# Rests of the query and up weights on GpSimd, gate columns and one scaling on ScalarE, and a new order of all steps, in a macaron transformer kernel

## What is computed

```python
x = x + 0.5 * _L0_ffn_ref(_layernorm(x), ...)
x = x + _L0_attn_ref(_layernorm(x), ...)
x = x + 0.5 * _L0_ffn_ref(_layernorm(x), ...)

def _L0_ffn_ref(x, ...):
    h = _rmsnorm(x, gamma1)
    q = (h @ Wq + bq).reshape(b, t, H, HD)                        # 16 heads of 16
    kv = ((h @ Wdown + bdown) @ Wup + bup).reshape(b, t, H, 2 * HD)  # 64 wide between
    k, v = jnp.split(kv, 2, axis=-1)
    att = softmax(jnp.einsum('bthd,btgd->bthg', q, k) / np.sqrt(HD))  # within one token
    x = x + (jnp.einsum('bthg,btgd->bthd', att, v).reshape(b, t, D) @ Wo + bo)
    h2 = _rmsnorm(x, gamma2)
    gate = softmax(h2 @ Wg + bg)
    return x + jnp.einsum('btd,edf,bte->btf', h2, We, gate)       # all 8 experts, dense

def _L0_attn_ref(x, ...):                                         # 8 heads of 32
    scores = jnp.einsum('bngh,bmgh->bnmg', q, k) / scale
    probs = softmax(scores, axis=-1)                              # over the heads
    return jnp.einsum('bnmg,bmgh->bngh', probs, v).reshape(b, n, d)
```

## Time and profile before

| | before |
|---|---|
| median of 3 runs | 992.51 us (992.35 to 993.81) |
| the profiled execution | 993.92 us, span of its profile 991.8 us |
| PE busy | 953.0 us (96%) |
| DVE busy | 854.7 us (86%) |
| POOL busy | 792.7 us (80%) |
| ACT busy | 642.2 us (65%) |
| granted clock of PE | 1.000 in every slice |

### The profile page before, as it was taken

The page is one execution under the profiler, slowest core; times in us unless marked ns, Lnnn a source line. Parts: engine busy times, 40 slices in busy tenths (PEclk is TensorE's granted clock), DMA queues, the critical chain, the costliest instruction groups (busy, mean ns, idle before and its releaser), DMA issues. The chain is left out here.

```text
span 991.8 us, 28114 instructions
## 1 busy us (share of the span) xinstructions
PE 953.0 (96%) x11052; PEld 755.2 (76%) x11052; DVE 854.7 (86%) x1388; ACT 642.2 (65%) x1287; POOL 792.7 (80%) x865
## 2 busy tenths in 40 slices
PE   8799999999999989999999999887999999999998
PEld 7678887888888866666666666456788888888886
DVE  6889999899785469999999999999998998898743
ACT  4677566565755467777877877776765765666542
POOL 6988887986885538999899999998778959968554
PEclk9999999999999999999999999999999999999999
DMA  7021000000000000000000000000000000000001
GB/s 226 3 76 45 2 2 2 2 2 2 2 1 1 1 1 2 2 2 2 1 2 2 2 1 2 2 1 2 2 2 22 23 3 22 2 24 22 2 23 42
DMA packets 8398, 14.45 MB, mean 15 GB/s; under 512 B 1993, under 2 KB 5964, under 8 KB 8270
## 3 DMA queue, kind: packets, MB, share of 16 engines
q1 hardware_dynamic: 8270, 12.67, 3.8%
HBM read 8.48 MB, written 4.19 MB: 13 GB/s over the span
## 5 line engine op out<-in xcount | busy, mean ns | idle before, releaser
L514 PE MATMUL psum<-we,h 128*128 128x512 f32 x1536 | 382.2, 399 | 1.6 <-DVE h L1219 1.6
L514 PEld LDWEIGHTS psum<-we,h 128*128 128x128 f32 x1536 | 280.9, 188 | 62.4 <-issue 1.7
L1422 ACT ACTIVATE late<-psum,gate 128x256 f32<-128x256 f32 x252 | 105.0, 469 | 104.2 <-PE psum L514 59.7
L1256 DVE SCALAR_TENSOR_TENSOR X<-psum,gate,X 128x256 f32<-128x256 f32 x260 | 124.0, 477 | 55.9 <-PE psum L514 42.1
L1282 DVE TENSOR_REDUCE oT<-psum 128x128 fp32r<-128x1024 f32 x128 | 154.9, 1218 | 12.9 <-PE psum L914 12.6
L1485 ACT ACTIVATE kvx<-psum 128x1024 f32<-128x1024 f32 x126 | 129.0, 1024 | 52.8 <-PE psum L924 42.2
L997 POOL TENSOR_TENSOR late<-kvx,late 128x2048 f32<-128x2048 f32 x31 | 121.5, 3920 | 35.5 <-ACT late L1492 24.8
L1288 DVE TENSOR_REDUCE late<-kvx 128x256 f32<-128x2048 f32 x63 | 143.4, 2276 | 0.0
L1645 POOL TENSOR_TENSOR late<-late 128x512 f32<-128x512 f32 x63 | 81.4, 1292 | 59.8 <-ACT late L1422 59.6
L997 POOL TENSOR_TENSOR kvx<-kvx,late 128x2048 f32<-128x2048 f32 x31 | 121.4, 3916 | 1.5 <-ACT late L1492 0.8
L1370 ACT ACTIVATE kvx<-kvcs,mask 128x512 f32<-128x512 f32 x132 | 89.5, 740 | 14.8 <-DVE kvcs L1131 8.5
(11 more groups left out here) (185 smaller groups left out, 1935.4 us busy)
## 6 DMA issues: line engine op xcount, KB each, us to landing
X<-in_L_attn_hidden_states SPq DMA_DIRECT2D x7, 512.0 KB, 6.0
out<-X SPq DMA_DIRECT2D x7, 512.0 KB, 2.6
X<-in_L_ffn_We SPq DMA_DIRECT2D x2, 1024.0 KB, 10.5
X<-in_L_attn_hidden_states SPq DMA_DIRECT2D x2, 256.0 KB, 2.9
out<-X SPq DMA_DIRECT2D x1, 384.0 KB, 2.3
late<-in_L_ffn_turned SPq DMA_DIRECT2D x1, 257.0 KB, 4.7
kvx<-in_L_ffn_Wq SPq DMA_DIRECT2D x1, 256.0 KB, 2.8
kvx<-in_L_ffn_Wup SPq DMA_DIRECT2D x2, 128.0 KB, 2.6
```

What stands on the lines that cost most here:

```text
L514: ins = e.matmul(out_ap, l, r, start=(n == 0), stop=(n == len(terms) - 1))
L1256: e.scalar_tensor_tensor(out=xi, in0=psum[:, u % 3, w * D:(w + 1) * D], scalar=gate[k % 2][:, i, 2 * n + w:2 * n + w + 1], in1=xi, op0=ALU ...
L1422: e.activation(y[:, n // 2 * 2 + w, :], psum[:, u % 3, w * D:(w + 1) * D], ACT.Copy, scale=gate[k % 2][:, i, 2 * n + w:2 * n + w + 1]).the ...
```

## The change

Six things: the rests of the query and up weights (`split_lo` 1 and 3) go from DVE to POOL, each with a semaphore of its own in place of counts of one; the two bias rows of the up weights stay on DVE as a step of their own (`bias_lo`); `gate_wo` goes from DVE to ACT, as three activations; `xs` of job 1 goes from POOL to ACT; the costs of these in the planner are set to match; and `SOONER`, `FIRST` and `SAME` are new numbers, which changes the order of nearly all steps. No instruction of the steady state is added or removed.

```diff
@@ -72,7 +72,7 @@
 
 def scaled_by_act(job, p, B):
 
-    return job == B or (job, p) == (0, 1)
+    return job in (1, B) or (job, p) == (0, 1)
 
 
 def parts_of(job, B):
@@ -103,9 +103,10 @@
         if n != 5:
             put("ACT", hi, ("split_hi", n), ("fold", n) if n < 2 else ("load", n), (None, ("gate_row", 0), None, None, ("gate_wo", 0))[n] if n < 5 else None)
         if n in (0, 1, 3):
-            put("DVE", lo, ("split_lo", n), ("split_hi", n))
+            put(*(("POOL", (0, 1770, 0, 2000)[n]) if n else ("DVE", lo)), ("split_lo", n), ("split_hi", n))
         elif n not in (2, 5, 6, 7):
             put("POOL", lo, ("rest_lo", n), ("split_hi", n))
+    put("DVE", 600, ("bias_lo", 0), ("split_hi", 2))
     put("SP", 4600, ("rows", 0))
     put("PE", 200, ("columns", 0), ("rows", 0))
     put("DVE", 150, ("mask", 0), ("columns", 0))
@@ -120,7 +121,7 @@
     put("DVE", 190, ("gate_row", 0), ("gate_last", 0), ("load", 1))
     put("SP", 12300, ("turned", 0))
     put("PE", 1350, ("gate_out", 0), ("gate_row", 0), ("turned", 0))
-    put("DVE", 400, ("gate_wo", 0), ("gate_out", 0), ("load", 4))
+    put("ACT", 850, ("gate_wo", 0), ("gate_out", 0), ("load", 4))
     for s in range(2 * B):
         split = parts_of(s, B)
         part = lambda p, s=s: p if parts_of(s, B) == 2 else 0
@@ -154,12 +155,12 @@
             put("ACT", 510, ("q_up", s, p), ("q_turn", s, p))
             put("POOL", 480, ("q_zero", s, p), ("q_up", s, p))
             put("PE", 488, ("key", s, p), ("la_lo", s, part(p)), ("la_one", s, part(p)), ("values", units - 2 * NT - 1) if s >= B else None,
-                *((f"key_{w}", c - 2) for w in "PA"), ("split_lo", 3))
+                *((f"key_{w}", c - 2) for w in "PA"), ("split_lo", 3), ("bias_lo", 0))
             put("DVE", 990, ("key_turn", s, p), ("key", s, p))
             for w, engine, ns in (("P", "POOL", 1405), ("A", "ACT", 2850 if c == 2 * B else 1270)):
                 if w == "A" or c != 2 * B:
                     put(engine, ns, (f"key_{w}", c), ("q_turn", s, p), ("key_turn", s, p), ("scores", c - 2),
-                        ("split_lo", 3), ("rest_lo", 4), ("normalise", units - 3) if c == 2 * B else None,
+                        ("split_lo", 3), ("bias_lo", 0), ("rest_lo", 4), ("normalise", units - 3) if c == 2 * B else None,
                         ("values", units - 1) if c == 2 * B + 1 else None)
             put("PE", 920, ("scores", c), *((f"key_{w}", c) for w in "PA"), ("q_zero", s, p), ("at", c - 2))
             put("DVE", 1390, ("top", c), ("scores", c), ("values", units - 2) if c == 2 * B else None)
@@ -171,12 +172,12 @@
                 put("ACT", 1050, ("la_v", s), ("la_lo", s, part(1)), ("val", s - 1))
                 put("POOL", 620, ("one_v", s), ("la_v", s))
                 put("PE", 1048, ("val", s), ("one_v", s), ("values", units - 2 * NT - 1) if s >= B else None,
-                    *((f"val_{w}", c - 3) for w in "PA"), ("split_lo", 3))
+                    *((f"val_{w}", c - 3) for w in "PA"), ("split_lo", 3), ("bias_lo", 0))
                 put("DVE", 1920, ("val_turn", s), ("val", s), ("normalise", units - 2) if s == B + 1 else None)
             for w, engine, ns in (("P", "POOL", 1405), ("A", "ACT", 2850 if c == 2 * B else 1270)):
                 if w == "A" or c != 2 * B:
                     put(engine, ns, (f"val_{w}", c), ("q_turn", s, p), ("val_turn", s), ("attend", c - 2),
-                        ("split_lo", 3), ("rest_lo", 4), ("normalise", units - 3) if c == 2 * B else None,
+                        ("split_lo", 3), ("bias_lo", 0), ("rest_lo", 4), ("normalise", units - 3) if c == 2 * B else None,
                         ("values", units - 1) if c == 2 * B + 1 else None)
             put("PE", 975, ("attend", c), ("at", c), *((f"val_{w}", c) for w in "PA"), ("mult", c - 1))
             put("DVE", 656, ("out_turn", c), ("attend", c), ("normalise", units - 1) if c == 2 * B else None)
@@ -283,25 +284,24 @@
-SOONER = {"key_A": 401506, "at_zero": 345096, "tokens": 316100, "gate_fold": 308394, "exp": 262595, "mask": 236826,
...
+SOONER = {"a_xs": 152625, "half": 142146, "one_v": 142082, "rms2": 135254, "mask": 130514, "tokens": 121416, "x1": 108804,
...
-FIRST = {0: 22566, 1: 48044, 2: 21974, 3: 22641, 4: -2645, 5: -29335, 6: -2913, 7: 47195}
-SAME = -12780
+FIRST = {0: 34958, 1: -15063, 2: 736, 3: 1062, 4: 760, 5: 542, 6: 666, 7: 10389}
+SAME = 4697
...
@@ -629,8 +630,8 @@
         def scaled(k, p):
 
             if scaled_by_act(k, p, B):
-                return s_xs_act, 1 if k == 0 else p + 2
-            return s_xs, 2 * k + p + (k == 0) - 2 * (k > B)
+                return s_xs_act, 1 if k == 0 else p + 2 + 2 * (k == B)
+            return s_xs, 1 if k == 0 else 2 * k + p - 2 - 2 * (k > B)
 
         def tiles_in(k, w):
 
@@ -775,7 +776,7 @@
                 elif name == "q":
                     p = piece[2]
                     if k == 0 and p == 0:
-                        e.wait_ge(s_lo, 2)
+                        e.wait_ge(s_lo_q, 1)
                     e.wait_ge(s_hT_lo, 2 * k + p + 1)
                     for i in (2 * p, 2 * p + 1):
                         ins = product(e, psum[:, b + i % 2, 0:D + E], three(hT, i, wq))
@@ -783,7 +784,8 @@
                 elif name == "key":
                     p = piece[2]
                     if k == 0 and p == 0:
-                        e.wait_ge(s_lo, 3)
+                        e.wait_ge(s_lo_kv, 1)
+                        e.wait_ge(s_lo_bias, 1)
                         e.wait_ge(s_const, 3)
                     e.wait_ge(s_la_one, done(k, p))
                     e.wait_ge(s_la_lo, done(k, p))
@@ -962,7 +964,10 @@
             k, p = c // 2, c % 2
             if c == 0:
                 e.wait_ge(s_consts_dve, 1)
-                e.wait_ge(s_lo, 3)
+                e.wait_ge(s_lo, 1)
+                e.wait_ge(s_lo_q, 1)
+                e.wait_ge(s_lo_kv, 1)
+                e.wait_ge(s_lo_bias, 1)
                 e.wait_ge(s_rest, 1)
             elif c > 1:
                 e.wait_ge(*((s_score, c - 1) if what == "key" else (s_attend, c - 1)))
@@ -1072,21 +1072,13 @@
                     e.wait_ge(s_glast, 1)
                     e.tensor_tensor(raw_q[:, :, D:], neg_g[:, :, :], psum[:, 2, 2 * E:3 * E].unsqueeze(1).to_broadcast([P, KC, E]),
                                     ALU.subtract).then_inc(s_grow, 1)
-                elif name == "gate_wo":
-                    e.wait_ge(s_gout, 1)
-                    e.wait_ge(l_bgate, 16)
-                    own.step(e.tensor_scalar(neg_b[:, 1, :], neg_b[:, 1, :], -1.0, None, ALU.mult))
-                    own.step(e.tensor_copy(neg_b[:, 0, :], psum[:, 2, 5 * E:6 * E]))
-                    e.tensor_copy(raw_o[:, :, D:], psum[:, 2, 3 * E:5 * E].rearrange("p (k n) -> p k n", k=KC)).then_inc(s_gwo, 1)
-                elif piece == ("split_lo", 0):
-                    split_lo(wd[:, :, 1, :], raw_d, wd[:, :, 0, :], s_fold, 1, 1)
-                elif piece == ("split_lo", 1):
-                    split_lo(wq[:, 1], raw_q, wq[:, 0], s_fold, 2, 2)
-                elif piece == ("split_lo", 3):
-
+                elif name == "split_lo":
+                    e.wait_ge(s_fold, 1)
+                    e.wait_ge(s_hi, 1)
+                    e.tensor_tensor(wd[:, :, 1, :], raw_d, wd[:, :, 0, :].bitcast(F32), ALU.subtract).then_inc(s_lo, 1)
+                elif name == "bias_lo":
                     e.wait_ge(s_hi, 3)
-                    own.step(e.tensor_tensor(wu[KVB, 1, :], raw_kvb, kvbhi, ALU.subtract))
-                    split_lo(wu[0:HALF, 1], raw_u[0:HALF, :], wu[0:HALF, 0], l_wu, 32, 4)
+                    e.tensor_tensor(wu[KVB, 1, :], raw_kvb, kvbhi, ALU.subtract).then_inc(s_lo_bias, 1)
                 elif name == "hT_lo":
                     p = piece[2]
                     cols = slice(2 * p * P, (2 * p + 2) * P)
@@ -1317,6 +1309,12 @@
                 elif piece == ("split_hi", 4):
                     e.wait_ge(s_gwo, 1)
                     split_hi(wo[:, 0], raw_o, l_wo, 16)
+                elif name == "gate_wo":
+                    e.wait_ge(s_gout, 1)
+                    e.wait_ge(l_bgate, 16)
+                    e.activation(neg_b[:, 1, :], neg_b[:, 1, :], ACT.Copy, scale=-1.0)
+                    e.activation(neg_b[:, 0, :], psum[:, 2, 5 * E:6 * E], ACT.Copy)
+                    e.activation(raw_o[:, :, D:], psum[:, 2, 3 * E:5 * E].rearrange("p (k n) -> p k n", k=KC), ACT.Copy).then_inc(s_gwo, 1)
                 elif name == "split_hi" and k >= 8:
                     n = AW_ORDER[k - 8]
                     split_hi(aw[n][:, 0], aw_raw[:, n], l_aw[n], 16)
@@ -1572,6 +1571,14 @@
                                     ALU.mult).then_inc(s_rs, 1)
                     e.wait_ge(own.sem, own.n)
                     e.tensor_tensor(r[:, 2, :], r[:, 2, :], r[:, 0, :], ALU.mult).then_inc(s_ratio, 1)
+                elif piece == ("split_lo", 1):
+                    e.wait_ge(s_fold, 2)
```

(6 more changed lines are left out.)

34 lines of the change are left out of this document (15 added, 19 removed).

## The result

| | before | changed |
|---|---|---|
| median | 992.43 us (992.32 to 993.81, 4 runs) | 997.95 us (997.13 to 998.16, 4 runs) |
| ratio | | 1.0047, 95% interval 1.0035 to 1.0059 |
| the profiled execution | 993.92 us, span 991.8 | 997.89 us, span 995.8 |

The change made the kernel 5.5 us slower; 2.4 us faster was forecast, and 995.8 was the top of the range. Both kernels were run once more as controls: 993.03 and 997.16 us, spans 990.9 and 995.5.

A forecast was written before the change was run, and what follows sets the result against it. PE bounds the kernel, busy 953.0 of 991.8 us. Startup -0.9, stalls -3.5, start of attention -0.3, array switches +0.6, handover +1.2 and steady jobs +0.5 sum to -2.4: 992.51 becomes 990.1 us, range 986.2 to 995.8.

The forecast's parts named there:

- Handover: Second pass taking over from attention: first expert of job 8 comes +1.2 us later, ends -1.4 and +2.5.
- at 16: DVE step at the handover, now behind top 17: from 682.81 to about 685.1, 2.3 us later, partly absorbed.
- Rival 2: Handover keeps normalise 63's early lead and one instruction stall is left: 986.3 us; chance 0.14.
- Stalls and steady jobs: PE's waits at instruction-block edges, five outside startup becoming two: -3.5 us; repeated order in the two passes: +0.5.
- the switches: Four more PE changes between whole array and tiles: +0.6 us, ends 0 and +1.6.
- 1218: Instruction-block edge on PE where a stall was expected to stay, because scores 2 are released late.
- 21442: Instruction-block edge on PE where a stall was expected to stay, because its pair begins with an attend.
- rival 3: Repeated order has one wait per steady job, attend behind scores or wo behind oT_lo: 996.6 us; chance 0.20.
- the first rival: PE's block-edge stalls: the five outside startup stay, no gain from them, sum +1.1, 993.6 us; chance 0.20.
- Startup: Reordered DVE and ACT work before the first expert: it starts 0.9 us sooner, ends -1.9 and +1.1.
- Start of attention: First batch's last value product behind the fourth qk covers PE's eviction wait: -0.3 us, ends 0 and -0.8.
- Slower: Outcome over 2 us slower than the kernel before: chance 0.20, of which 0.18 from rival 3.

The follow-up runs named there:

- e15: Changed kernel with POOL's second x1_base of job 8 moved ahead of normalise 62, as in the kernel before; 996.08 us, ratio 1.0034.
- e4: Kernel before with five expert products moved into its chains of scores and attends, one for each stall outside startup; 990.98 us, ratio 0.9979.
- e14: Kernel before with only the expert product ahead of scores 31 moved; 991.63 us, ratio 0.9988.
- e10: Changed kernel's order until mid attention, order before from there, plus one expert product moved ahead of scores 31; 991.48 us, ratio 0.9982 to the kernel before.
- e2: Changed kernel with the old SOONER, FIRST and SAME numbers, so old order with new engines; 998.88 us, ratio 1.0055 to the kernel before.

## Why the prediction was wrong

Between the controls the change cost 4.7 us of span where a gain of 2.4 was forecast. Of these 7.1 us, 3.1 lie in the handover and 1.9 each in the first pass and in startup.

- **Handover, forecast +1.2, measured +4.3 and +5.2: the step that failed.** It has two parts. First, "POOL's x1_base ... will be held in the same way": the competition was seen, its winner was taken over from the earlier trace rows, and it went the other way. DVE lost 3.3 us, and values 63 and scores 17 with it: from values 56 to scores 17 +1.1 us in the controls and +1.7 in the first pair, of which e15 gives 1.5 back (33.49 for 34.95). Second, at 16: forecast 2.3 us later, measured 3.9 in the controls and 4.7 in the first pair, counted from values 56. The delay of attend 16 behind scores 17 was +2.9 (4.65 for 1.80), and from there to the first expert nothing was absorbed (18.58 for 18.20), where I had counted on half. Rival 2 was wrong at the same place.
- **Stalls and steady jobs, forecast -3.5 and +0.5 (with the switches +1.1).** The count of instructions named the edges rightly, and e4, e14 and e10 show that the stalls go when the chain is cut. The two stalls expected to stay were 1218 (it did, in most profiles) and 21442 (it did not). Between the controls 2.5 us of stalls went from the first pass, and it got only 1.1 shorter; 1.0 went from the second, and it got 0.5 longer. What was missed is mostly a wait once per job, rival 3's mechanism at another place: the prediction has key_P done "some 2.5 us ahead" of the pairs, and PE waits for it ahead of scores in nine jobs. These are 1.0 us in the first pass of the control and 0.7 in the second; waits of the same size for DVE add 0.5 in the first. In the second pass PE is also busy for 0.8 us more; whether that is the price of the switches no run here shows.
- **The Trainium skill's rule** (Runtime: NRT & Kernel Launch, Instruction fetch mechanics) that crossing a block is mostly hidden was the first rival. The traces speak against it in chains of short matmuls (e2: 1.57 us of idle time at one edge). For the whole time the rule (no gain from them, 993.6) would have misled less than the sum did, because other waits took up much of the gain.
- **Startup, forecast -0.9, measured +1.0 and +1.9.** The walk gave at 1 and the first x1 within 0.3 us of before; attend 1 was 1.3 late in the controls. The walk missed that key_A 0 behind xs of job 1 holds scores 0, and that scores 1 shares a PSUM bank with scores 0. The ends (-1.9 and +1.1) held the controls' value only.
- **Start of attention (-0.3) and attention:** within 0.1 us of nothing.
- **The chances.** "Slower" stood on one mechanism (0.20), rival 3. It happened, but with 0.2 us per job and not 0.7; it alone would not have made the kernel slower, and the sign came from the handover and startup. The handover's upper end (+2.5) was the cost if nothing of the at 16 delay is absorbed; the hold of DVE by POOL was in no end of it, though the earlier trace rows showed both engines at the place.

## What to carry to other kernels

When two engines that hold each other are brought to a new overlap, the trace of the old overlap does not tell which of them will lose: bound the cost by the whole of the other's work for either, and ask which of the two is on the path. An idle stretch of the fullest engine is worth at most its length, and a new order that removes it may bring small waits of its own: where a pattern repeats in every job, read for one job how far ahead each of its inputs is ready, before the gain is booked. Numbers that set an order fit the costs and engines that they were tuned with, so such a change is tested whole, or by splicing the orders at a point where all engines meet.

## What the hardware showed that was not expected

- Which of DVE and POOL is held is not always settled by who began first. For `normalise` 63 DVE began first each time. The x1_base of POOL that began 0.63 to 0.68 us later held it in all seven profiles that have it there (7.09 to 7.28 us for 3.8); adds that began 1.2 and 2.4 us later were held themselves (3.6 and 2.89 us for 1.28). Elsewhere in the same profiles the earlier one did win: in the control of the kernel before, DVE's L1211 began at 303.80, and POOL's L1627, begun 0.25 us later, took 1.06 us where its usual is 0.20. So the later start alone is not what decides, and what does was not tried further. The memsets ran at full pace beside DVE.
- Whether PE stalls at the edge of a block is told by when the packet starts against the chain, not by the chain's length: 252 instructions cost 0.2 to 0.9 us, 174 cost 0.8 to 1.2 (19650 and 1218, in different orders).
- In startup the profile's granted clock and PE's pace did not agree: the pace rose only after some 20 us, also where 1.00 was shown from the first slice (kernel before: twelve query matmuls took 2.99 us at 16.43 and 1.83 at 20.06). So startup's clock was not used as a cause here, apart from the filler transposes, whose durations (4.29 for 2.84 us, 24 of them) speak for themselves.
